# Gate-weight combinations on GpSimd in four operations of 1024 columns, and the first group's tile sums put between the two combinations

## The reference

```python
w_bot = einsum('bg,got->bot', cond_8, weight * mask[None])      # (2, 512, 512)
h = einsum('bnt,bot->bno', x, w_bot) + bias                     # x: (2, 2048, 512)
def bitlinear(x, w):      # activations rounded to 8 bits per row, weights to -1, 0, 1
    return einsum('bsi,oi->bso', act_quant(x), weight_quant(w))
gate, up = silu(bitlinear(h, w_gate)), bitlinear(h, w_up)       # (2, 2048, 2048)
return x + bitlinear(gate * up, w_down)
```

## Time and profile before

| | |
|---|---|
| median of 3 runs | 433.60 us (432.94 to 434.90) |
| time of the profiled execution | 433.37 us |
| its span, first to last instruction | 431.6 us |
| granted TensorE clock, mean over the span | 1.00 |
| busy: PE, DVE, ACT, POOL | 420.2, 355.1, 305.3, 324.0 us |
| PE busy share of the span | 97% |

### The profile page before, as it was taken

One profiled execution on the slowest core, in us unless ns is written; L12 is line 12 of the kernel. 1 busy time (PEld: TensorE's weight loads), 2 busy tenths in 40 slices (PEclk: granted clock), 3 DMA queues, 4 the chain that ended last, 5 costly groups with the idle time before them and its releaser, 6 DMA issues.

```text
span 431.6 us, 7666 instructions
## 1 busy us (share of the span) xinstructions
PE 420.2 (97%) x2282; PEld 255.6 (59%) x2282; DVE 355.1 (82%) x593; ACT 305.3 (71%) x459; POOL 324.0 (75%) x306
## 2 busy tenths in 40 slices
PE   4899999999999999999999999999999999999997
PEld 0233588888855465555656556656655655655554
DVE  1236778888897898899999999999999999999891
ACT  1214998788887885877768786777868668786842
POOL 0005999999408999898779796887979779796872
DMA  7999999995213344445555445453354453444766
GB/s 273 404 400 409 295 360 305 306 303 152 59 27 73 62 109 100 134 112 120 102 119 99 133 98 132 110 114 97 97 147 111 108 122 97 111 104 126 114 153 174
DMA packets 104462, 69.84 MB, mean 162 GB/s; under 512 B 87280, under 2 KB 87536, under 8 KB 102896
## 3 DMA queue, kind: packets, MB, share of 16 engines
q1 hardware_dynamic: 103712, 67.13, 57.9%
q10 hardware_dynamic: 720, 2.36, 1.5%
HBM read 40.11 MB, written 8.39 MB: 112 GB/s over the span
## 4 chain that ended last, share of the span: by engine, by line
PE 85%; POOL 9%; DMA 2%; DVE 2%; issue 1%; ACTq 0%; POOLq 0%; DVEq 0%
PE ps L1457 27%; PE ps L1497 18%; PE ps L1577 15%; PE ps L1414 10%; PE ps L1355 7%; PE ps L1404 2%; PE ps L1512 2%; DMA wc<-wcond 2%; PE ps L1368 2%; POOL wc L470 1%; POOL wc L475 1%; POOL wc L473 1%; POOL wc L471 1%; PE ps L1522 1%; POOL gcombo L397 1%
## 5 line engine op out<-in xcount | busy, mean ns | idle before, releaser
L1152 DVE TENSOR_TENSOR wc<-ps,xT_sb 128x512 f32<-128x512 f32 x104 | 69.0, 682 | 5.7 <-issue 2.3
L1497 PE MATMUL ps<-wc 128*128 128x256 f16 x448 | 58.1, 273 | 0.3 <-DVE wc L1105 0.3
L715 ACT ACTIVATE xT_sb<-ps,gate_unit 128x512 f32<-128x512 f32 x78 | 50.5, 685 | 9.2 <-PE ps L1457 8.4
L1186 DVE TENSOR_REDUCE p_part<-wc 128x1 f32<-128x1024 f32 (+2 forms) x42 | 50.9, 1211 | 0.4
L1497 PEld LDWEIGHTS ps<-wc 128*128 128x128 f16 x448 | 43.8, 98 | 12.4 <-issue 0.7
L1414 PE MATMUL ps<-tern_up,qT 128*128 128x512 f16 x192 | 49.3, 379 | 0.0
L486 POOL TENSOR_TENSOR result<-result,x_res 128x512 f32<-128x512 f32 x14 | 18.2, 1301 | 38.1 <-issue 38.1
L1497 PE MATMUL ps<-tern_down,wc 128*128 128x256 f16 x336 | 43.5, 273 | 0.0
L735 ACT ACTIVATE wc<-wc 128x1024 f16<-128x1024 f32 x38 | 39.8, 1051 | 1.6 <-DVE wc L1289 1.2
L1497 PEld LDWEIGHTS ps<-tern_down,wc 128*128 128x128 f16 x336 | 32.9, 98 | 12.8
L720 ACT ACTIVATE wc<-wc,p_scale 128x2048 f32<-128x2048 f32 x18 | 36.0, 2001 | 5.7 <-DVE p_scale L1280 5.7
(11 more groups left out here) (164 smaller groups left out, 1047.2 us busy)
## 6 DMA issues: line engine op xcount, KB each, us to landing
xT_sb<-xT SPq DMA_DIRECT2D x32, 256.0 KB, 5.8
x_res<-x SPq DMA_DIRECT2D x30, 256.0 KB, 3.0
out<-result SPq DMA_DIRECT2D x29, 256.0 KB, 2.0
wc<-wcond SPq DMA_DIRECT2D x12, 512.0 KB, 13.3
wc<-w_gate SPq DMA_DIRECT2D x4, 1024.0 KB, 14.7
wc<-w_up SPq DMA_DIRECT2D x4, 1024.0 KB, 8.1
wc<-w_down SPq DMA_DIRECT2D x4, 1024.0 KB, 6.6
wc<-wcond ACTq DMA_DIRECT2D x4, 512.0 KB, 7.7
```

The source lines that it names most:

```text
L715: nc.scalar.activation(gsilu[:, q, i % 2], source, ACT.Silu, scale=unit_column(s + i // 2)).then_inc(gsilu_ready[q], 1)
L1152: nc.vector.tensor_tensor(prod[:, par, 512 * i:512 * i + 512], up, source, ALU.mult).then_inc(prod_ready, 1)
L1186: nc.vector.tensor_reduce(p_part[:, par, i:i + 1], prod[:, par, 512 * lo:512 * hi], AX.X, ALU.max, apply_absolute_value=True).then_inc(par ...
L1497: ins = nc.tensor.matmul(ps[:, bank, cut], tile, weight, start=(i < (2 if apart(j) else 1) and k == 0), stop=(k == KB - 1), skip_group_che ...
```

## The change

`combine_gate(q)` no longer loops over two halves of the rows of weights: each of the four combinations is now one operation of 128x1024 where it was two of 128x512. There are 8 operations in all instead of 16. The two tile sums of group 0 that stood in the loop's step t = 4 are moved ahead of `combine_gate(0)`, in step t = 2. On PE, the first group's products of quarters 0 and 1 wait for the combination that each of them reads (1, 3 or 4 operations done) where the first product waited for all eight.

```diff
@@ -388,15 +388,14 @@
                 combos, done = gcombo[q], gcombo_ready[q]
                 pool.wait_ge(tern_done, PIECES)
                 pool.wait_ge(cond_psum, LATE - 2 if q == 0 else TILES)
-                for k in range(2):
-                    b11, b12 = tern_gate[:, q, k], tern_gate[:, q + 2, k]
-                    b21, b22 = tern_gate[:, q, 2 + k], tern_gate[:, q + 2, 2 + k]
-                    nc.gpsimd.tensor_tensor(combos[:, 0, k], b12, b11, ALU.subtract).then_inc(done, 1)
-                    nc.gpsimd.tensor_tensor(combos[:, 2, k], b22, b12, ALU.subtract).then_inc(done, 1)
-                    pool.wait_ge(done, 4 * k + 1)
-                    nc.gpsimd.tensor_tensor(combos[:, 1, k], b22, combos[:, 0, k], ALU.subtract).then_inc(done, 1)
-                    pool.wait_ge(done, 4 * k + 3)
-                    nc.gpsimd.tensor_tensor(combos[:, 3, k], b21, combos[:, 1, k], ALU.subtract).then_inc(done, 1)
+                b11, b12 = tern_gate[:, q, 0:2], tern_gate[:, q + 2, 0:2]
+                b21, b22 = tern_gate[:, q, 2:4], tern_gate[:, q + 2, 2:4]
+                nc.gpsimd.tensor_tensor(combos[:, 0], b12, b11, ALU.subtract).then_inc(done, 1)
+                nc.gpsimd.tensor_tensor(combos[:, 2], b22, b12, ALU.subtract).then_inc(done, 1)
+                pool.wait_ge(done, 1)
+                nc.gpsimd.tensor_tensor(combos[:, 1], b22, combos[:, 0], ALU.subtract).then_inc(done, 1)
+                pool.wait_ge(done, 3)
+                nc.gpsimd.tensor_tensor(combos[:, 3], b21, combos[:, 1], ALU.subtract).then_inc(done, 1)
@@ -562,7 +561,7 @@
                 if t % 2 == 0:
-                    if GSTEP - 2 <= t:
+                    if GSTEP <= t:
                         add_tiles((t - GSTEP + 2) // 2, 0)
                         add_tiles((t - GSTEP + 2) // 2, 1)
@@ -582,6 +581,8 @@
                 if t == 2:
+                    add_tiles(0, 0)
+                    add_tiles(0, 1)
                     combine_gate(0)
@@ -1427,11 +1428,12 @@
                     elif first:
-                        pe.wait_ge(gcombo_ready[q], 8)
                         pe.wait_ge(cond_shared_out, LAST_PAIR - PAIR0 + 1)
                         pe.wait_ge(silu_ready, 4 * GSTEP - 4)
                     else:
                         pe.wait_ge(gsilu_ready[q], 4 * g - 1)
+                if first and q < 2 and i in (0, 3, 6):
+                    pe.wait_ge(gcombo_ready[q], {0: 1, 3: 3, 6: 4}[i])
```

## The result

| | before | after |
|---|---|---|
| median | 433.60 us (13 runs, 432.88 to 435.44) | 436.08 us (13 runs, 434.02 to 438.51) |
| profiled execution | 433.37 us, span 431.6 | 434.02 us, span 432.2 |
| mean granted TensorE clock | 1.00 in the profiled one; the others' isn't on record | seven 0.999 or 1.000, six 0.995 or 0.996 |

The ratio is 1.0050, 95% interval 1.0029 to 1.0072: slower by 0.5%, where 0.33% was forecast. The medians by themselves lie 2.48 us apart, 0.57%.

What follows compares the result with a forecast made beforehand. PE was taken to pace the kernel to the end. Removing its tile-sum wait (−0.38) and delaying up chunk (4,0) (+1.82) gave +1.44 us on 433.37, a median of 435.0 us, range 433.4 to 436.4.

Steps and rivals of the forecast that it cites:

- What bounds the kernel: PE paces the kernel to the end; any delay of it around 150 to 170 us arrives undiminished.
- The tile sums, −0.38 us: Sums moved ahead of quarter 0's combination remove PE's 0.38 us idle before the first group product at 169.60.
- The finer waits, 0: PE's waits per combination matter only if `combine_gate` is late at the first group product; worth 0.
- The four wide operations, +1.82 us: GpSimd's 1024-column operations shut DVE out longer; `product(3, 2)` and PE's up chunk (4,0) come 1.82 us later.
- the upper end of 2.30: Longest expected 1024-column GpSimd operation, twice 1.15 us; 2.13 was taken, and the upper end adds 0.5 us.
- The fourth `add_blocks`: DVE operation at 159.55, meeting quarter 0's operations: at worst 0.95 us more, within 1.75 and 2.9 us slack; priced 0.
- Rivals 1, 2 and 3: 1: wait goes, nothing replaces it, 0.12; 2: DVE misses a boundary, 437.1 us, 0.06; 3: later slack used up, 0.14.
- The sum, +1.44 us: −0.38 + 1.82 on the profiled 433.37 us gives 434.81; expected median 435.0 us, +0.33%.
- the forecast's own 434.2 to 435.8: Forecast's own range, chance 0.68, covering both operation lengths and the 0.38 us gained or not.
- rival 3: After the fourth `add_blocks`, slack is used up and PE waits at `down_product(0, 5)`: 435.5 to 436.5 us; chance 0.14.
- the whole range of 433.4 to 436.4: Predicted range for the median that leaves out the first two rivals, together 0.18.
- The change part by part: Prediction's section pricing each edit; behind up chunk (4,0) it has all engines shifted with PE, with no new waits.

Runs made afterwards that it cites:

- four operations only: Kernel before with only the four 1024-column operations per combination; tile sums where they were, PE waiting for all four: 434.59 us against 433.29, ratio 1.0031.
- the kernel with PE's gap filled: Changed kernel with gate chunk (4,0) made three times, useless matmuls where PE was idle: 434.65 us, ratio 1.0025 to the kernel before.
- the four kernels without that wait: Order and finer waits only, 0.9981; changed kernel with GpSimd waiting for DVE, 0.9975, DVE's third sum later, 0.9973, or narrower operations (256/512 columns), 0.9973.

## Why the prediction was right, and what it missed

**What bounds the kernel.** Right. PE took every delay and every gain of this stretch to the end; after the group product no wait of PE followed in either kernel.

**The tile sums, −0.38 us.** The wait is gone, and on PE's path that was worth 0.56 us. The list counts idle time from the end of the four matmuls ahead, 1.03 us behind their start, while undisturbed the next group starts after 0.87; so the distance between two starts was the better measure. But the gain is not the move's: with four operations only the wait vanished without it, since PE came later. The move and the finer waits earned something by themselves with narrow operations alone, 0.46 us in the median.

**The finer waits, 0.** True for the changed kernel. For the move without the wide operations they carry 0.84 us, by the estimate above.

**The four wide operations, +1.82 us.** Right in mechanism, place and size: +1.82 at the product and +1.83 at PE. The pair of line 1105 took 4.54 us (4.56 by the prediction's times), a 1024-column operation 2.13 us and 2.57 when held. The estimate of 2.22 us from the Trainium skill, GPSIMD Engine Reference, section 3.1, and the upper end of 2.30 were both too long. The fourth `add_blocks` met a whole operation: 2.53 us in place of 1.69, 0.84 more of the 0.95 allowed, and PE didn't wait for it, as the slack said. Rivals 1, 2 and 3 didn't occur: PE had its new wait, DVE got in at every boundary at which it waited, and no wait of PE followed.

**The sum, +1.44 us.** The path in the profile gave +1.27, the kernel with PE's gap filled +1.28. The measured median was +2.5 us. 436.08 lies outside the forecast's own 434.2 to 435.8; it falls among rival 3's 435.5 to 436.5, though rival 3 didn't happen, and inside the whole range of 433.4 to 436.4. That it does is luck: none of these was made for a lower clock. The step that failed is "The change part by part", the sentence "Behind this, DVE, ACT and GpSimd are all shifted with PE, and nothing new is waited for": it treated a wait as costing its own length. A wait with 1.95 us of idle put PE 1.83 us behind and, in 12 of 25 executions, brought about 1.7 us of lower clock on top. The median of 436.08 sits among those executions.

Nothing in the one profile of the kernel before had shown such a cost. The 5.6 us of waiting in the earlier trace rows are the start of the span, before PE's first matmul; the longest wait behind work is one of 1.64 us that ends at 16.48, in every kernel here, and the matmuls behind it run at full speed. The start does show slow matmuls, but not in the clock:

```profile
L1368 PE MATMUL ps<-wc,mix_w x64: 592/593/1062, 5.6 to 35.0; 128*32 128x512 f32 x64
```

Up to about 13 us a matmul of this line takes 1.06 us (the maximum of the row), later 0.59 (its median), and the granted clock reads 1.00 in both stretches.

Why four operations alone had the low clock in 2 of 12 executions and the changed kernel in 12 of 25, with the same idle time, is open; with these counts it may be chance.

## To carry to other kernels

Where GpSimd and DVE work on SBUF operands side by side, the length of one GpSimd operation is the longest time that DVE can be held up at each of its own, so merging GpSimd's operations is paid for by DVE: before merging, look at which DVE operation that can be held (here those with two operands in SBUF, and one with a single operand) stands ahead of what PE needs next, and how much slack that has. The cure can be on any of three sides: narrower operations, GpSimd waiting until DVE is through, or the DVE operation moved behind the urgent one; each of them turned a loss of 2.5 to 2.6 us in the median into a gain of 0.8 to 1.0. A wait of PE of some 2 us can cost more than its length, and a profile of one execution may not show it: compare the mean clocks of many.

## What the runs showed of the hardware

- The granted clock fell to 1.2 GHz about a microsecond after PE had taken up work again, behind an idle time of 2.15 us, and was back about 3.5 us later, with PE at work throughout. One trace shows this. A mean clock of 0.996 or less, which is what such a fall gives, stood in 22 of 49 timed executions of the kernels with 1.94 to 2.15 us of idle there (6 of 13, 6 of 12, 2 of 12, 8 of 12), in none of 47 of the four kernels without that wait, none of 12 with the gap filled, none of 70 of the kernel before.
- The granted clock doesn't show every slow stretch: it reads 1.00 in the first 13 us, where a matmul of line 1368 takes 1.06 us in place of 0.59.
- An `add_blocks` of DVE that waits for GpSimd ends 0.53 to 0.56 us after GpSimd's operation, whether that has 256, 512 or 1024 columns; GpSimd's next takes 0.33 to 0.45 us more (2.46 or 2.58 in place of 2.13).
- Two DVE operations without a semaphore between them passed in one gap between GpSimd's operations (0.53 us on GpSimd for both).
